# Three graph layers of a GNN kernel with the product turned: parts of h stationary, counts of several destination blocks moving

## The reference

```python
for l in range(3):
    msg = h[src] + h_edge_attr
    agg = segment_sum(msg, dst)
    out = agg + h
    z = layernorm(out @ W1[l].T + b1[l], g1[l], be1[l])
    z = gelu(z, approximate=False)
    z = layernorm(z @ W2[l].T + b2[l], g2[l], be2[l])
    h = gelu(z + h, approximate=False)
```

## Time and profile before

| | us |
|---|---|
| median of 3 runs | 4917.65 (4916.52 to 4917.86) |
| the profiled execution | 4921.67 |
| its span in the profile | 4919.9 |
| mean granted clock of PE in it | 0.959 |

### The profile page before, as it was taken

The page is one execution under the profiler, slowest core; times in us unless marked ns, Lnnn a source line. Parts: engine busy times, 40 slices in busy tenths (PEclk is TensorE's granted clock), DMA queues, the critical chain, the costliest instruction groups (busy, mean ns, idle before and its releaser), DMA issues. The chain is left out here.

```text
span 4919.9 us, 112691 instructions
## 1 busy us (share of the span) xinstructions
PE 4234.3 (86%) x38465; PEld 3838.6 (78%) x38465; DVE 3072.4 (62%) x7967; ACT 1933.2 (39%) x4103; POOL 2466.8 (50%) x2823
## 2 busy tenths in 40 slices
PE   1499999999976788888888888889889998888997
PEld 1499999999965677777787777778785666888886
DVE  6799999999734444444444444444454445888887
ACT  1556666566522222212212222222134444555666
POOL 5511111111057777777777777777721002665564
PEclk9799999999989999999999999999999999999998
DMA  5444554455555666766766766677675555666665
GB/s 116 176 196 196 217 213 196 199 215 212 207 138 138 173 202 205 206 199 201 210 199 199 207 204 208 195 211 207 200 218 190 183 186 199 210 208 211 223 213 170
DMA packets 571499, 966.86 MB, mean 197 GB/s; under 512 B 101223, under 2 KB 418775, under 8 KB 552519
## 3 DMA queue, kind: packets, MB, share of 16 engines
q1 hardware_dynamic: 407520, 767.32, 44.5%
q0 software_dynamic: 60048, 125.37, 10.2%
q10 hardware_dynamic: 103767, 72.40, 5.6%
HBM read 707.25 MB, written 257.60 MB: 196 GB/s over the span
## 5 line engine op out<-in xcount | busy, mean ns | idle before, releaser
L1049 POOL DMA_INDIRECT ACC<-table,BIG x1715 | 1688.7, 985 | 625.8 <-issue 516.8
L1849 PE MATMUL ps<-BIG 128*128 128x257 f32 x3430 | 864.1, 395 | 154.7 <-ACT BIG L1289 153.9
L2481 DVE TENSOR_TENSOR BIG<-ps,ACC 128x512 f32<-128x512 f32 (+1 forms) x441 | 297.9, 675 | 1102.6 <-DMA ACC<-table,BIG 941.3
L1849 PEld LDWEIGHTS ps<-BIG 128*128 128x128 f32 x3430 | 634.1, 195 | 260.3 <-ACT BIG L1289 178.3
L1289 ACT ACTIVATE BIG<-BIG 128x512 f32<-128x512 f32 (+1 forms) x441 | 273.6, 620 | 1336.8 <-DVE BIG L2481 1324.5
L1864 PE MATMUL ps<-H_R,EXACT 128*128 128x256 f32 x4802 | 634.6, 288 | 97.7 <-DVE EXACT L2671 65.7
L1579 PE MATMUL ps<-H,ACC 128*128 128x128 f32 x4802 | 689.9, 284 | 0.0
L1864 PEld LDWEIGHTS ps<-H_R,EXACT 128*128 128x128 f32 x4802 | 591.9, 192 | 122.2 <-DVE EXACT L2671 88.5
L1579 PEld LDWEIGHTS ps<-H,ACC 128*128 128x128 f32 x4802 | 588.0, 191 | 0.2 <-ACT ACC L1230 0.2
L1230 ACT ACTIVATE BIG<-ps 128x392 bf16<-128x392 f32 x784 | 390.3, 498 | 466.7 <-PE ps L1565 466.7
L1104 POOL CAST EXACT<-X 128x768 fp32r<-128x768 bf16 (+1 forms) x392 | 366.1, 937 | 283.0 <-PE ps L1864 263.7
(11 more groups left out here) (294 smaller groups left out, 8025.2 us busy)
## 6 DMA issues: line engine op xcount, KB each, us to landing
weight_mat<-ACC SPq DMA_DIRECT2D x49, 3136.0 KB, 9.2
BIG<-in_edge_attr SPq DMA_DIRECT2D x392, 256.0 KB
X<-count_mat SPq DMA_DIRECT2D x98, 800.0 KB, 4.4
count_mat<-BIG SPq DMA_DIRECT2D x49, 1568.0 KB, 12.8
X<-count_mat SPq DMA_DIRECT2D x98, 768.0 KB, 4.3
REL_WT<-weight_mat SPq DMA_DIRECT2D x275, 256.0 KB
BIG<-rel_tab ACTq DMA_DIRECT2D x392, 128.0 KB
BIG<-weight_mat SPq DMA_DIRECT2D x176, 256.0 KB
```

The costliest lines, as they stand in the source:

```text
L1049: pool.indirect_dma_start(GR[:, q * QUAD + u, :], None, tables[1], bass.IndirectOffsetOnAxis(ap=STEP_IDX[:, b % 3, r * QUAD + u:r * QUAD + ...
L1849: mm = pe.matmul(PS[4 + par][:, 0:HIW], DR[:, q * QUAD + u, :], HB[:, q * QUAD + u, :], start=(r == 0 and u == 0), stop=(r == QB - 1 and u ...
L2481: dve.tensor_tensor(HB[:, steps, 0:F], PS[n % 2][:, 0:size * F].rearrange("p (u f) -> p u f", f=F), GR[:, own, :], ALU.add).then_inc(rows_ ...
```

## The change

- The product is turned. A 128x128 part of h, float32r, is stationary; the counts move, float32r, for a *superblock* of 4 (ten of them) or 3 (three) destination blocks, 512 or 384 columns. An *item* is one source block of one superblock: two matmuls, one for each part of h. The sum comes out turned, so the transpose before W1 goes; the own row and attribute sum are added by a matmul with the identity.
- All three layers hold h in two float32r parts. ACT makes the high part, DVE the low part, in `H_R`.
- SP loads the counts as pieces of four source blocks (rows of 4 x 128 bf16 values) for all blocks of a superblock, six buffers `RAW` in `X`. An item's counts, one run of 128 out of each of the 4 or 3 destination blocks, are converted into one of seven slots, by ACT for slots 0, 2, 4, 6 and by DVE for 1, 3, 5. POOL converts nothing.
- The node chain works on superblocks, its steps set at fixed positions (`LAG_OF`, counted in items behind the superblock's end), all in programs without loops. The root is a guess from the bits and three Newton steps on DVE.
- The first two superblocks of a layer are interleaved (10 pieces, 4, 3, 9), so that the last blocks of the layer before are needed late.
- The count products between the window products go; windows have other buffers (`FW_BIG`, `FW_ACC`, four of them in turn from window 12 on); the first four pieces of counts are loaded between windows (`FINAL_PIECES`); x is stored by ACT's queue in seven pieces; POOL moves 11 of 13 chunks of the attribute sums earlier; the output is stored in six pieces.

```diff
+FW_SLOT = list(range(10)) + [4, 5] + [6 + w % 4 for w in range(FWINS - 12)]
+FINAL_PIECES = {15: 0, 17: 1, 21: 2, 24: 3}
+SIZES_OF_SB = [4] * 10 + [3] * 3
+RAWS = 6
+CSLOTS = 7
+CSLOTS_OF_ACT = (0, 2, 4, 6)
+FIRST_SPLIT, SECOND_SPLIT = 10, 4
+CHAIN = 38
+OWN_SUMS = [40 if g == 0 else SB_END[g - 1] + 12 for g in range(SB_COUNT)]
+LAG_OF = {"sum_turned": 4, "z": 5, "z_bias": 9, "z_stats": 10, "z_moments": 12, "z_guess": 14, "z_root1": 15, "z_root2": 16, "z_root3": 17, "z_norm": 18,
+          "z_turned": 20, "z_gelu": 23, "y": 25, "y_bias": 29, "y_stats": 31, "y_moments": 33, "y_guess": 34, "y_root1": 35, "y_root2": 36,
+          "y_root3": 37, "y_norm": 39, "y_scale": 41, "y_add": 43, "out": 45, "high": 46, "low": 48}
...
+            def load_piece(n):
...
+                sp.dma_start(RAW[n % RAWS][:, 0:nb * rows * P].rearrange("p (b c) -> p b c", b=nb),
+                             count_mat[own, :, k * PIECE * P:(k * PIECE + rows) * P].rearrange("b p c -> p b c")).then_inc(raw_in[n % RAWS], 16)
...
+            def item(i):
...
+                to, counts = PS[g % 2][:, 0:nb * P], COUNTS[i % CSLOTS][:, 0:nb * P]
+                pe.matmul(to, H_R[l][:, h, 0, :], counts, start=(i == SB_START[g]), stop=False)
+                pe.matmul(to, H_R[l][:, h, 1, :], counts, start=False, stop=False).then_inc(counts_used, 1)
+                if at == SB_END[g]:
+                    pe.wait_ge(own_ready, g + 1)
+                    for j in range(nb):
+                        mm = pe.matmul(PS[g % 2][:, j * P:(j + 1) * P], SB_SUM[:, j, :], ident[:, :], start=False, stop=(j == nb - 1))
+                    mm.then_inc(csum_ps, 1)
...
+            def converted(i):
...
+                if i >= CSLOTS:
+                    dve.wait_ge(counts_used, i - CSLOTS + 1)
+                dve.tensor_copy(slot_counts(i), raw_counts(i)).then_inc(dve_converted, 1)
...
+            def root_guess(g, name, k):
...
+                step(name + "_var", g, dve.tensor_scalar(nmr[:, cols], MV[:, cols, 1], EPS, None, ALU.add))
+                stepped(name + "_var", g)
+                step(name + "_root0", g, dve.tensor_scalar(rstd[:, cols].bitcast(I32), nmr[:, cols].bitcast(I32), -0.5, float(0x5f3759df), ALU.mult, ALU.add))
+            def root_step(g, name, k, n):
...
+                step(name + "_t1", g, dve.tensor_tensor(rcnt[:, cols], rstd[:, cols], nmr[:, cols], ALU.mult))
+                stepped(name + "_t1", g)
+                step(name + "_t2", g, dve.scalar_tensor_tensor(rcnt[:, cols], rcnt[:, cols], -0.5, rstd[:, cols], ALU.mult, ALU.mult))
+                stepped(name + "_t2", g)
+                step(f"{name}_root{n}", g, dve.scalar_tensor_tensor(rstd[:, cols], rcnt[:, cols], 1.5, rstd[:, cols], ALU.add, ALU.mult))
...
+                for pos in range(LAYER_END):
+                    if pos < len(ITEMS) and pos % CSLOTS not in CSLOTS_OF_ACT:
+                        converted(pos)
+                    if pos in OWN_SUMS:
+                        own_sums(OWN_SUMS.index(pos))
+                    for g in behind(pos, "z_bias"):
+                        bias(g, "z", 0, SB_ZY, 4, L_B1[g // SBS], z_ps, z_sum)
...
-            def count_products(l, par, k, first, last):
-                for h in range(first, last):
-                    mm = pe.matmul(PS[par][:, 0:3 * F], CIN[k][:, h * P:(h + 1) * P], HP0[:, h, :, :].rearrange("p k f -> p (k f)"),
-                                   start=(h == 0), stop=(h == BLOCKS - 1))
...
```

More of the change, by code:

```diff
@@ L153 @@
 ALL_NODE_USES = len(NODE_USES)
[L154 to L159, removed]
+SIZES_OF_SB = [4] * 10 + [3] * 3
+SBS = len(SIZES_OF_SB)
+SB_AT = [sum(SIZES_OF_SB[0:s]) for s in range(SBS + 1)]
+SB_OF = [s for s in range(SBS) for _ in range(SIZES_OF_SB[s])]
@@ new lines, in sb_z @@
+            def sb_z(g):
+                l, nb, own = of_sb(g)
+                if g % SBS == 0:
+                    pe.wait_ge(layer_in, LAYERS * 128 if l else 128)
+                pe.wait_ge(oT_sb, g + 1)
+                if g == 0:
+                    pe.wait_ge(fin_free, FIN0 + C1)
+                else:
+                    pe.wait_ge(z_sum, g)
+                for j in range(nb):
+                    mm = pe.matmul(PS[4][:, j * P:(j + 1) * P], SB_SUM[:, j, :], L_W1[l], start=True, stop=True)
+                mm.then_inc(z_ps, 1)
@@ L2011, in general_layers @@
+            def dense_layers():
+                for pos in range(LAYER_END):
+                    if pos in Z_AT:
+                        sb_z(Z_AT[pos])
+                    for g in behind(pos, "z_turned"):
+                        sb_z_turned(g)
+                    for g in behind(pos, "y"):
+                        sb_y(g)
+                    if pos < len(ITEMS):
+                        item(pos)
             def general_layers():
@@ new lines, in stepped, with over_nodes, own_sums @@
+            def stepped(name, g):
+                dve.wait_ge(node_step, step_of[name, g])
+            def over_nodes(row, nb):
+                return row.rearrange("p (a f) -> p a f", a=1).broadcast_to([P, nb, F])
+            def own_sums(g):
+                l, nb, own = of_sb(g)
+                if g == 0:
+                    dve.wait_ge(attr_moved, C1)
+                else:
+                    dve.wait_ge(z_ps, g)
+                if l:
+                    dve.wait_ge(gelu_done, g - SBS + 1)
+                elif g == 0:
+                    dve.wait_ge(newh, BLOCKS + C1)
+                dve.tensor_tensor(SB_SUM[:, 0:nb, :], H[:, own, :], T1[:, own, :], ALU.add).then_inc(own_ready, 1)
+                if g % SBS == 0:
+                    dve.wait_ge(layer_in, LAYERS * 128 if l else 128)
+                step("shift", g, dve.tensor_tensor(H[:, own, :], H[:, own, :], over_nodes(L_BE2[l], nb), ALU.add))
@@ new lines, in bias, with sb_stats @@
+            def bias(g, name, k, array, bank, row, ready, free):
+                l, nb, own = of_sb(g)
+                dve.wait_ge(ready, g + 1)
+                if g and name == "z":
+                    dve.wait_ge(yn_ready, g)
+                dve.tensor_tensor(array[:, 0:nb, :], PS[bank][:, 0:nb * P].rearrange("p (b f) -> p b f", f=F), over_nodes(row, nb), ALU.add).then_inc(free, 1)
+            def sb_stats(g, name, k, array, summed):
+                l, nb, own = of_sb(g)
+                dve.wait_ge(summed, g + 1)
+                for j in range(nb):
+                    ins = dve.bn_stats(ST[:, k + j, :], array[:, j, :])
+                step(name + "_stats", g, ins)
```

527 lines of the change are left out of this document (249 added, 278 removed).

## The result

The changed kernel takes 4790.14 us (median of 4 runs, 4784.44 to 4792.51), the kernel before 4917.75 on the same chip: a ratio of 0.9738 with a 95% interval of 0.9721 to 0.9755. The forecast was 4766 with a range of 4618 to 4880. The profiled execution took 4790.99 us for a span of 4789.2.

A forecast was written before the change was run, and what follows sets the result against it. Layer 0 was taken as bound by PE alone, layers 1 and 2 also by DVE's conversions. Start 3693 + layers 353.7 + 353.7 + 342 + tail 26 = 4768 us span, median 4766 us, range 4618 to 4880.

The forecast's parts named there:

- 60, 63, 20 and 9 us: Forecast gains: layer 0; layer 1 with its changeover; the start and the gap behind layer 0; layer 2 and the tail.
- Matmul: Float32r product in the layers: 0.219 us for 512 columns, 0.165 for 384; bounds for 512 were 0.213 and 0.227.
- rival (a): Layers: PE bound, the slots cover DVE's bursts; 301.5 us a layer, median 4621; chance 0.22.
- Waits: PE idle per superblock of 4: z 2.3 us, y 0.6, output 1.0; 24.6 + 3.9 = 28.5 us.
- e+19: Item 19 behind a superblock's end; its conversion follows z's normalisation, 8.4 us after the z products; PE arrives after 6.1.
- The superblock of 3: Superblock of 3 blocks: PE alone 18.5 us, waits 2.2 + 1.2 + 1.0, together 22.9 us.
- rival (b): DVE's conversions at half rate: superblocks of 31.6 and 25.2 us, median 4879; only 3 blocks, some 20 us; chance 0.11.
- Layer 2: Last layer: 353.7 us less 7 for no high part and 4.4 for no items behind its last superblock: 342.
- Start: Ahead of layer 0: window products 58.4 us from 3628.6, then a gap of 6; PE starts layer 0 at 3693.
- Tail: After the layers, the last node chain, store and end: 26 us, 28.9 before.
- (c): Rival on count loads: 1 KB pieces land too slowly; at 100 ns a packet the span is 5160; chance 0.06.
- (d): Rival on weights: loads not hidden beside running matmuls; superblocks of 42.6 and 36.6 us, kernel 5326; chance 0.01.

The follow-up runs named there:

- e_no_conv: Changed kernel without conversions behind the first seven items and count loads behind the first six pieces, to time TensorE alone: 4677.2 us (one run).
- e_own_late: Changed kernel with VectorE's own sum and shift 24 items, not 12, behind the end of the superblock before: 4752.68 us, 0.9663 of the kernel before.
- e_high_late: Changed kernel with ScalarE's high part moved from item 46 to 50 and VectorE's low part from 48 to 52: 4779.75 us, 0.9717 of the kernel before.
- e_cast4: Changed kernel with VectorE converting four runs of 128 for superblocks of 3 too: 4779.13 us, 0.9715 of the kernel before.
- e_pool_spread: Changed kernel with GpSimd's last-layer output sums each waiting only for their own part of x: 4790.91 us, 0.9735 of the kernel before.

## Why the prediction was right

**The cause was the one forecast; that the sum came so close was in part luck.** TensorE's own work per layer fell to some 319 us (10 x 25.9 + 3 x 20.0, by e_no_conv), and what is left above it are waits for conversions that the written order makes late; e_own_late and e_high_late each moved one piece of work and took its waits away (all but 0.17 us a superblock behind z). Of the forecast's 60, 63, 20 and 9 us came 57, 61, 18 and -6 with the cuts of the earlier trace rows. With layer 1 cut where it ends, the same forecast says 60, 33, 20 and 38 (layer 2 and tail), and 57, 32, 18 and 24 came. The sum of the forecast does not hang on that cut.

**Two terms inside a superblock were off and cancelled.** *Matmul:* taken at 0.219, bounds 0.213 to 0.227; it is 0.228 to 0.233, above the upper bound. The nearest row, 257 float32 columns, gave too little; 0.013 of overhead on 256 float32r columns was the better guide. It makes PE alone 25.9 and 20.0, not 24.6 and 18.5, and puts rival (a)'s 4621 out of reach: without waits for conversions the kernel takes 4677. *Waits:* 3.9 us forecast, 2.3 found (28.2 - 25.9). By starts of matmuls, z cost 1.5 against 2.3, y nothing against 0.6, the output 0.6 against 1.0. VectorE took 7.7 us from the end of the z products (4163.0) to the conversion of e+19 (4170.7, a tenth ahead of the late matmul) where 8.4 were counted, and PE, slower by its matmul, came after 6.4 and not 6.1. The errors are 1.3 and 1.6 us, and the sum, 28.5, hit 28.2 because they have opposite signs. (The conversion of four runs, taken at 0.33, was right: two such in a row start 0.33 apart.)

**The superblock of 3** (22.9 forecast, 25.2 measured) failed at its conversion, 0.265 taken for 384 columns: they are 545 ns busy, the half-rate case that rival (b) allowed for 3 blocks, with some 20 us. Of the 2.3 us, 1.1 are PE's own and 0.4 the wait for z's normalisation that stays without conversions (20.0 against 18.5); e_cast4 gave 1.4 a superblock back, 13 us in all.

**Layer 2** was the step that failed most: 342 forecast, 357.0 measured. GpSimd's five sums in a row cost 5.9 us, from an operation the forecast had named and priced at nothing. Without them (e_pool_spread) layer 2 takes 352.2 against 355.0 for layer 1. Since PE's own time is 3.0 more in layer 2 (319.64 against 316.62 in e_no_conv), the missing high part gave some 5.8 of the 7 us counted; and the 4.4 for a last superblock with no items behind it did not come: its predecessor's chain still runs beside it, and what runs dry lies in the tail.

**Start:** 3693 forecast, 3694.87 measured, from two errors again. The window products began 6.7 us before; in the thirteen profiles they begin anywhere from 3618.99 to 3629.50, and the 3628.60 of before lie among these, so no effect of the change is shown in it. The gap was 14.3 us, not 6: 2.1 for a store to wait for, and 3.8 us of "issue", for which the forecast had no term, and 2.4 not resolved. A row of before that it did not read has 3.02 us of the same kind, on VectorE at the same place:

```profile
3703.85 0.29 DVE L2681 TENSOR_TENSOR NODE<-H,T 128x128 f32<-128x128 f32 x1 [3.02 <-issue]
```

The window products took 58.6 (58.4 forecast). **Tail:** 25.9 for 26.

**The rivals.** (a) is out of reach, as said. (b) held for 3 blocks only. (c): no wait of ScalarE or VectorE for raw counts in the layers, a piece lands in 4.8 us, DMA busy 0.75 to 0.78. (d): weight loads of 0.19 us stay hidden beside matmuls 0.23 apart.

**What the sum did not ask** is what the two smaller parts of the change are worth. "ScalarE's roots and table loads go for nothing: its idle time hid them" was right, and said half: the steps that replace them are not hidden. They are eleven dependent operations on the engine that is late, in the stretch where it is late, and undoing them alone gives 46 us; a seventh of the conversions on GpSimd gives some 28. So the rest of the change brings the gain, and these two parts give back some of it. How the gain divides among the turned product, the two parts of h instead of three in layer 0 and the order at the changeovers was not tried.

## What to carry to other kernels

Where engines run fixed programs, look behind each wait for what stands ahead of the late operation on its engine: moving 1.4 us of work per superblock that nobody needs yet took 37 us off. Work taken off an idle engine to save its overhead costs if it lands on the one that is late; price it by the wait in its stretch and not by mean load. And a wait put down to one engine can start on another, one step further back.

## What the runs showed of the hardware that was not expected

- VectorE's root steps on 4 columns took 1.14 to 1.22 us instead of 0.16 while GpSimd added 512 columns, each about as long as one of GpSimd's five sums (6.22/5 = 1.24); when the burst ended they were fast again. The Trainium skill, "Advanced Engine Details and Errata", section "GPSIMD Details", says that the Pool engine shares a read and a write interface with VectorE and conflicts with its instructions with two SBUF inputs; the slow steps are of that kind, and the trace agrees.
- A conversion of three runs of 128 is slower (545 ns) than one of four (425).
- A float32r matmul of 512 columns follows the last after 0.228 to 0.233 us whether or not conversions run; the first after an idle stretch or a node group takes some 0.1 more. Layer 1, whose parts of h lie in another tile (H_ACC), is the quicker one, 316.62 us against 319.64 in e_no_conv; why stays open.
- Between the last chunk and the first instruction of the layers ScalarE and VectorE issue nothing for 3.8 to 4.0 us, and the profile shows nothing that they wait for. In the trace both run a compare-and-branch of line 706 (the choice between the two ways through the kernel) at either end of that time (ScalarE at 3689.99 and 3693.94); what fills it was not tried.
